# Repeated waits for a semaphore's value left out in an attention and FFN kernel

## The chip, the core and the metric

One NeuronCore of a Trainium2 chip runs the whole kernel. The metric is the device time of one execution in microseconds (us), lower is better. The engines are PE (TensorE), DVE (VectorE), ACT (ScalarE), POOL (GpSimd) and SP (SyncE, which here only issues DMAs). Each runs its own program, and they are ordered against each other by semaphores alone.

## What is computed

```python
# x: 2 x 1024 x 256, ctx: 2 x 77 x 256, all float32, 16 heads of 16
n   = layernorm(x)                                  # no scale, no shift
q   = n @ Wq + bq;  k = ctx @ Wk + bk;  v = ctx @ Wv + bv
att = 0.25 * q k^T per head
att = softmax(att * mask - 1e10 * (1 - mask))       # mask: 1 x 1 x 1024 x 77
x   = x + (att @ v) @ Wo + bo
n   = layernorm(x)
y   = n + relu(n @ w1[0] + b1[0]) @ w2[0] + b2[0]   # only expert 0 has weight
x   = x + layernorm(y) * gamma + beta
```

## The kernel before

The 2048 rows of x are worked off in four chunks of 512 rows (c = 0 to 3). A chunk goes through these kinds of steps: norm and scale (DVE, the first layernorm), turn (PE transposes, L557), qproj (the q projection, L573 and L574), smax (L643, 12 steps: scores with 128 rows of x as the stationary side, whose maximum over the 77 keys DVE takes at L978), mxt (the transposed maxima), st (L663, 16 steps, one a head: scores in the transposed layout, which ACT exponentiates at L824), pv (L675, four heads at a time), weigh, attn, proj (L702, L704, L707, the output projection), turn2 (L716), ffn1 (L725 to L727, 8 steps), ffn2 (L739, L740, L742, 8 steps), and result, root and finish (the last layernorm). A float32 operand that goes into a fast matmul is split into a high and a low part, so ffn1 and ffn2 use three matmuls for each product.

The order of the work is fixed. A table of planned times per engine (TIMES) lists every step, and walk(engine) returns that engine's steps sorted by it. So chunks overlap: while ffn1 and ffn2 of one chunk run, score steps of the next are put between them. Each engine's program loops over its walk and writes, in front of a step's instructions, a wait for each thing that the step needs: the semaphore and the value that it must have reached. The values come from the step's number (nth) and only grow. A step states all its needs, also those that an earlier step of the same engine has stated. A score step on PE reads:

```python
e.wait_ge(sq_ld[u % 2], 32 * (u // 2 + 1))
e.wait_ge(sq_static, 8 + 16 * (c // 2))
e.wait_ge(ks_made, 6)
e.wait_ge(ks_ident, 4)
if nth[step] > 2:
    e.wait_ge(exped, nth[step] - 2)
```

An engine instruction (a matmul, a copy, the issue of a DMA) can carry one wait itself. The others of the same step stand before it in separate semaphore instructions of the engine's sequencer, with up to two waits in each; the profile has them as EVENT_SEMAPHORE at the line of a wait (L660, L662 for the score step, L636, L637, L639 for smax, L671 and L673 for pv, L738 for ffn2, L540 for a PSUM bank that is taken).

SP's program issues the transfers: the first loads, and for each chunk quadq (L519: q of four heads, from the scratch tensor qD in DRAM, into four slots of the tile Sq), quadm (L528: the negated maxima, nmx, into one row of the same slots), qload (L510 and L512: q into the tile Mq), and qproj (L500, L502: the high and low part of q out to qD). masks (L493) loads the mask part of Sq once for the second half (1280 KB). Sq has two halves of four slots, and a half is loaded again once PE's scores have read it: this is the wait for st_made at L518 and L527. finish stores the result.

Of the kernel before, what the change touches and what calls it, by code (L numbers as in the profile page):

```python
# [211 lines left out]


# [6 lines left out]
def build(nc, x, ctx_in, mask, Wq, bq, Wk, bk, Wv, bv, Wo, bo, w1, b1, w2, b2, gamma, beta, const, out):  # L220
    stack = ExitStack()
    with stack:
# [236 lines left out]
        def sync_program(e):  # L459
            e.dma_start(xin[:, 0:4, :], x_v[:, 0:4, :]).then_inc(ld_x[0], 16)  # L460
# [9 lines left out]
            for step in walk("SP"):  # L470
# [11 lines left out]
                elif kind == "statics":  # L482
                    e.wait_ge(mT_made, 1)
                    e.dma_start(mD[:, :], mT[:, :].bitcast(F32)).then_inc(m_out, 16)
                elif kind == "maskm":
                    e.wait_ge(m_out, 16)
                    e.wait_ge(scored, 24)
                    e.dma_start(Mqf[0:QR, :, :], mD[:, 512:1024].unsqueeze(1).to_broadcast([QR, 6, 512])
                                ).then_inc(ms_static, 16)
                elif kind == "masks":  # L490
                    e.wait_ge(m_out, 16)
                    e.wait_ge(st_made, 32)
                    e.dma_start(Sqf[0:QR, :, :], mD[:, 512:1024].unsqueeze(1).to_broadcast([QR, 8, 512])  # L493
                                ).then_inc(sq_static, 16)
                elif kind == "qproj":
                    c, g = a
                    qd = qD[c][8 * g:8 * g + 8]
                    e.wait_ge(q_high, nth[step])
                    for r in (0, 2):
                        e.dma_start(qd[:, r, :, :], qh[:, g, :].bitcast(F32)).then_inc(q_out[g], 16)  # L500
                    e.wait_ge(q_split, nth[step])
                    e.dma_start(qd[:, 1, :, :], ql[:, g, :].bitcast(F32)).then_inc(q_out[g], 16)  # L502
                elif kind == "qload":
                    c, g = a
                    e.wait_ge(q_high, nth[step])
                    if c:

                        e.wait_ge(scored, 12 * (c - 1) + (12 if g else 8))
# [4 lines left out]
                elif kind == "quadq":  # L513
                    c, k = a
                    u, s = quad(c, k), 4 * (k % 2)
                    e.wait_ge(q_out[k // 2], 48 * (c + 1))
                    if u > 1:
                        e.wait_ge(st_made, 4 * (u - 1))  # L518
                    e.dma_start(Sqf[QR:P, s:s + 4, :],  # L519
                                qD[c][4 * k:4 * k + 4].rearrange("h r d n -> (r d) h n")).then_inc(sq_ld[u % 2], 16)  # L520
                elif kind == "quadm":
                    c, k = a
                    u, s = quad(c, k), 4 * (k % 2)
                    e.wait_ge(nmx_made, nth["mxt", c, k // 2])
                    if u > 1:
                        e.wait_ge(st_made, 4 * (u - 1))
                    e.wait_ge(sq_static, 8 + 16 * (c // 2))  # L527
                    e.dma_start(Sqf[MR:QR, s:s + 4, :], nmx[s:s + 4, k // 2, :].bitcast(F32)).then_inc(sq_ld[u % 2], 16)  # L528
                elif kind == "finish":
                    c, h, na, nb = a  # L530
                    n0 = row0(c) + 2 * h + na
                    e.wait_ge(y_done, nth[step])
                    e.dma_start(o_v[:, n0:n0 + nb - na, :], xn2[:, c % 2, 2 * h + na:2 * h + nb, :]).then_inc(stored[h], 16)
            for h in range(2):
                e.wait_ge(stored[h], 16 * (NC + 1))

        def tensor_program(e):
            def take(key):
                if free_when[key]:
                    e.wait_ge(*free_when[key])  # L540
                return bank[key]

            for step in walk("PE"):
                kind, a = step[0], step[1:]
                if kind == "rows":
                    e.wait_ge(ld_rows, 64)
                    e.wait_ge(ld_c, 16)
                    t = bank[step]
                    e.transpose(t[:, 0:14], rows[:, :], cst[0:14, 0:14]).then_inc(rows_turned, 1)
                elif kind == "turn":  # L550
                    c, = a
                    e.wait_ge(x_normed, nth["scale", c])
                    e.wait_ge(ld_c, 16)
# [5 lines left out]
                elif kind == "ctx":  # L559
                    e.wait_ge(ld_ctx, 16)  # L560
                    e.wait_ge(ld_c, 16)
# [6 lines left out]
                elif kind == "qproj":  # L568
                    c, g = a
                    e.wait_ge(xnT_made, 2 * nth["turn", c])  # L570
                    e.wait_ge(ld_wq, 16)
# [4 lines left out]
                elif kind == "kproj":  # L576
                    g, = a
                    e.wait_ge(ctx_made, 1)
                    e.wait_ge(ld_wk, 16)
# [5 lines left out]
                elif kind == "keys":  # L585
# [3 lines left out]
                    e.wait_ge(sel_made, 5)  # L589
                    e.wait_ge(low_ident, 1)  # L590
                    e.wait_ge(*((cols_made, 1), (ctx_made, 1), (v_copied, 1), (v_copied, 2), (mT_made, 1), (ks_made, 1),
                                (ks_made, 3), (ks_made, 4))[nth[step] - 1])
                    e.wait_ge(k_split, g + 1)
                    e.wait_ge(bqk_split, 1)
# [12 lines left out]
                elif kind == "bqk":  # L607
                    e.wait_ge(k_raw, 2)
                    e.wait_ge(bqh_made, 1)
# [5 lines left out]
                elif kind == "mask":  # L615
                    e.wait_ge(crow_made, 3)
                    e.wait_ge(identb_made, 1)
# [3 lines left out]
                elif kind == "values":  # L621
                    b, = a
                    e.wait_ge(ctx_made, 1)
                    e.wait_ge(ld_wv, 16)
# [3 lines left out]
                elif kind == "smax":  # L628
# [3 lines left out]
                    for g in (0, 1) if s == 2 else (s,):  # L632
                        e.wait_ge(ms_ld[g], 48 * (c + 1))
                    e.wait_ge(ms_static, 6 + 16 * (c // 2))
                    e.wait_ge(km_made, 6)
                    e.wait_ge(km_ident, 1)  # L636
                    e.wait_ge(ks_made, 2)  # L637
                    if nth[step] > 2:
                        e.wait_ge(maxed, nth[step] - 2)  # L639
# [6 lines left out]
                elif kind == "mxt":  # L646
                    c, g = a
                    e.wait_ge(maxed, 12 * c + (12 if g else 8))
# [4 lines left out]
                elif kind == "st":  # L653
# [3 lines left out]
                    e.wait_ge(sq_ld[u % 2], 32 * (u // 2 + 1))  # L657
                    e.wait_ge(sq_static, 8 + 16 * (c // 2))
                    e.wait_ge(ks_made, 6)
                    e.wait_ge(ks_ident, 4)  # L660
                    if nth[step] > 2:
                        e.wait_ge(exped, nth[step] - 2)  # L662
                    e.matmul(T[(nth[step] - 1) % 2][0:TK, :], KS[:, h, b, :], Sq[:, h % 8, :],  # L663
                             start=True, stop=True).then_inc(st_made, 1)
                elif kind == "pv":
# [3 lines left out]
                    e.wait_ge(exped, 4 * (u + 1))  # L669
                    e.wait_ge(v_copied, 2)  # L670
                    e.wait_ge(cleared, 3)  # L671
                    if u:
                        e.wait_ge(pv_copied, u)  # L673
# [4 lines left out]
                elif kind == "weigh":  # L678

                    c, k = a  # L680
                    e.wait_ge(pv_copied, nth[step])
# [4 lines left out]
                elif kind == "attn":  # L686
                    c, g = a
                    e.wait_ge(weighed, nth["weigh", c, 2 * g + 1])
# [4 lines left out]
                elif kind == "proj":  # L693
                    c, = a
                    e.wait_ge(wo_split, 1)
                    for h in range(2):
                        t = take(step + (h,))
                        for n in range(2):
                            q = (2 * h + n) * 128
                            for k in range(2):  # L700
                                e.wait_ge(a_high, nth["attn", c, k])
# [4 lines left out]
                                e.wait_ge(a_split, nth["attn", c, k])  # L706
# [3 lines left out]
                elif kind == "turn2":  # L710
                    c, = a
                    e.wait_ge(x2_normed, nth["scale2", c])
# [5 lines left out]
                elif kind == "ffn1":  # L718
                    c, f = a
                    e.wait_ge(x2_split, 2 * nth["turn2", c])  # L720
                    e.wait_ge(w1_split, 4)
# [7 lines left out]
                elif kind == "ffn2":  # L729
                    c, h, part = a  # L730
                    e.wait_ge(w2_split, 4)
# [5 lines left out]
                    for f in range(first, first + 4):  # L737
                        e.wait_ge(h_high, nth["ffn1", c, f])  # L738
                        e.matmul(y, hh[:, f, q:q + 128], w2h[:, f * E:(f + 1) * E], start=(f == 0), stop=False)  # L739
                        e.matmul(y, hh[:, f, q:q + 128], w2l[:, f * E:(f + 1) * E], start=False, stop=False)  # L740
                        e.wait_ge(*low_eng[c, f])
# [4 lines left out]
        def scalar_program(e):  # L746
            e.dma_start(ctx[:, :, :], ctx_in.rearrange("b t e -> t b e")).then_inc(ld_ctx, 16)
# [461 lines left out]
```

## Time and profile before

| | |
|---|---|
| median of 3 runs | 252.32 us |
| lowest and highest run | 250.85 and 252.41 us |
| profiled execution, first to last instruction (its span) | 250.3 us |
| the profiled execution's own time | only its span is given; the runs above are others |
| instructions in the span | 4118 |
| busy: PE, PE weight loads | 210.7 us (84%), 161.1 us (64%) |
| busy: DVE, ACT, POOL | 149.8 (60%), 121.3 (48%), 80.4 us (32%) |
| moved by DMA | 26.12 MB in 18101 packets |

The profile is of one execution. Busy time is that of the engine itself; time of its sequencer, on separate waits or on issuing a DMA, is not in it. Consecutive matmuls overlap in the records, so a matmul's duration is longer than the distance to the next; the chain of waits shows that distance. In the chain, "issue" is time for which the profile shows no wait, and a name with a q (SPq) is that engine's sequencer.

### The profile page before, as it was taken

To read this page: it belongs to the slowest core of one execution; us is meant where nothing else is said; L and a number is where in the kernel's file an instruction comes from. 1 tells how busy PE (TensorE), PEld (TensorE's weight loads), DVE (VectorE), ACT (ScalarE), POOL (GpSimd) and SP (SyncE) were. 2 spreads that over 40 slices of the span, in tenths; PEclk is the share of its full clock that TensorE was granted. 3 is DMA by queue.
4 is the path that set the end of the run, shared out by engine and by line. 5 is a ranking of instruction groups with operands and counts; after the bars stand their busy time and mean duration, and the time that the engine had idled before them with its cause. 6 is when DMAs were issued, how large, how long until landed. Compare 5 with 4: busy or idle time off the path is not lost.

```text
span 250.3 us, 4118 instructions
## 1 busy us (share of the span) xinstructions
PE 210.7 (84%) x1273; PEld 161.1 (64%) x1273; DVE 149.8 (60%) x354; ACT 121.3 (48%) x210; POOL 80.4 (32%) x88
## 2 busy tenths in 40 slices
PE   0378787687598687996999999999999999979990
PEld 0264765354434574474869776889677889968790
DVE  0988759764464477343136966745776426886464
ACT  2445921363376127768351547773646870149200
POOL 5629507310301031524121352241371341370010
PEclk9999955979799889999799999999999999999999
DMA  7962589347947636396044344000330100011011
GB/s 179 351 210 65 167 225 265 113 131 228 199 94 179 178 106 125 92 198 160 0 99 137 67 105 107 0 3 4 72 98 4 42 0 3 0 42 45 0 43 42
DMA packets 18101, 26.12 MB, mean 104 GB/s; under 512 B 2441, under 2 KB 9393, under 8 KB 18081
## 3 DMA queue, kind: packets, MB, share of 16 engines
q1 hardware_dynamic: 17200, 25.05, 38.8%
q10 hardware_dynamic: 881, 0.82, 1.3%
q8 instruction: 11, 0.18, 0.3%
q14 instruction: 9, 0.07, 0.1%
HBM read 14.92 MB, written 8.72 MB: 94 GB/s over the span
## 4 chain that ended last, share of the span: by engine, by line
PE 50%; DMA 18%; SPq 11%; DVE 11%; issue 7%; ACT 1%; POOL 1%; POOLq 0%; DVEq 0%
DMA Sq<-nmx 6%; PE W L725 5%; PE W L727 5%; PE W L726 5%; PE T L663 5%; DMA qD<-ql 4%; SPq L510 4%; PE W L742 4%; PE W L739 4%; PE W L740 4%; PE acc L675 4%; DMA Sq<-mD 3%; SPq L500 3%; PE W L557 2%; DMA Sq<-qD 2%
## 5 line engine op out<-in xcount | busy, mean ns | idle before, releaser
L824 ACT ACTIVATE PT<-T 77x512 f32<-77x512 f32 x64 | 35.2, 590 | 33.5 <-PE T L663 31.8
L739 PE MATMUL W<-w2h,hh 128*128 128x256 f32 x128 | 36.9, 288 | 0.4 <-ACT hh L868 0.4
L742 PE MATMUL W<-w2h,hl 128*128 128x256 f32 x128 | 36.4, 285 | 0.2 <-DVE hl L1041 0.2
L740 PE MATMUL W<-w2l,hh 128*128 128x256 f32 x128 | 36.3, 283 | 0.0
L978 DVE TENSOR_REDUCE mx<-M 128x6 f32<-128x462 f32 (+1 forms) x48 | 26.3, 581 | 15.4 <-PE M L643 14.6
L663 PE MATMUL T<-Sq,KS 128*77 128x512 f32 x64 | 25.4, 456 | 5.3 <-DMA Sq<-nmx 3.0
L864 ACT ACTIVATE hr<-W,cols 128x512 f32<-128x512 f32 x32 | 22.0, 688 | 14.3 <-PE W L727 13.1
L725 PE MATMUL W<-x2h,w1h 128*128 128x512 f32 x64 | 26.5, 414 | 1.5 <-DVE x2l L1035 1.5
L1159 POOL TENSOR_TENSOR hl<-hr,hh 128x512 fp32r<-128x512 f32 x12 | 15.5, 1288 | 34.7 <-ACT hh L868 34.7
L1041 DVE TENSOR_TENSOR hl<-hr,hh 128x512 fp32r<-128x512 f32 x20 | 14.5, 727 | 20.1 <-ACT hh L868 20.0
L643 PE MATMUL M<-KM,Mq 128*128 128x234 f32 (+1 forms) x96 | 21.0, 337 | 6.4 <-issue 2.3
L739 PEld LDWEIGHTS W<-w2h,hh 128*128 128x128 f32 x128 | 24.5, 192 | 2.1 <-issue 0.8
L727 PE MATMUL W<-x2h,w1l 128*128 128x512 f32 x64 | 25.7, 402 | 0.0
L726 PE MATMUL W<-x2l,w1h 128*128 128x512 f32 x64 | 25.6, 400 | 0.0
L643 PEld LDWEIGHTS M<-KM,Mq 128*128 128x128 f32 (+1 forms) x96 | 17.2, 229 | 12.7 <-issue 8.4
L740 PEld LDWEIGHTS W<-w2l,hh 128*128 128x128 f32 x128 | 24.5, 191 | 0.6
L742 PEld LDWEIGHTS W<-w2h,hl 128*128 128x128 f32 x128 | 24.4, 191 | 0.4 <-DVE hl L1041 0.4
L1129 POOL TENSOR_TENSOR xin<-xin,bo_r 128x512 f32<-128x512 f32 x8 | 10.6, 1342 | 37.4 <-DVE xn L916 37.4
L868 ACT CAST hh<-hr 128x512 fp32r<-128x512 f32 x32 | 19.8, 620 | 1.0
L1165 POOL TENSOR_TENSOR rs<-ve,mh 128x2 f32<-128x2 f32 (+1 forms) x10 | 6.4, 641 | 42.3 <-DVE ve L1062 42.1
L663 PEld LDWEIGHTS T<-Sq,KS 128*77 128x77 f32 x64 | 9.2, 155 | 14.9 <-issue 8.4
L675 PE MATMUL acc<-PT,Vb 77*32 77x512 f32 x128 | 17.2, 610 | 0.0
(138 smaller groups left out, 413.5 us busy)
## 6 DMA issues: line engine op xcount, KB each, us to landing
Sq<-qD SPq DMA_DIRECT2D x16, 384.0 KB
qD<-qh SPq DMA_DIRECT2D x16, 256.0 KB
xin<-in_x_dram SPq DMA_DIRECT2D x4, 512.0 KB, 9.4
qD<-ql SPq DMA_DIRECT2D x8, 256.0 KB
Mq<-qh SPq DMA_DIRECT2D x16, 96.0 KB, 3.8
out_dram<-xn SPq DMA_DIRECT2D x6, 256.0 KB, 2.4
Sq<-mD SPq DMA_DIRECT2D x1, 1280.0 KB, 8.2
w1raw<-in_L_ffn_w_dram SPq DMA_DIRECT2D x2, 512.0 KB, 8.8
```

What stands on the lines that cost most here:

```text
L643: i = e.matmul(m[:, j * w * KP:(j + 1) * w * KP], Mq[0:r, 2 * s + j, n * 128:(n + 1) * 128], KM[0:r, h0:h0 + w, b, :], start=True, stop=True)
L663: e.matmul(T[(nth[step] - 1) % 2][0:TK, :], KS[:, h, b, :], Sq[:, h % 8, :], start=True, stop=True).then_inc(st_made, 1)
L675: i = e.matmul(acc[32 * j:32 * j + 32, :], Vb[:, b, 4 * k + j, :], PT[:, (4 * u + j) % 6, :], start=True, stop=True, tile_position=(0, 32 ...
L725: e.matmul(t[:, :], w1h[:, o:o + 128], x2h[:, k, :], start=(k == 0), stop=False)
L726: e.matmul(t[:, :], w1h[:, o:o + 128], x2l[:, k, :], start=False, stop=False)
L727: i = e.matmul(t[:, :], w1l[:, o:o + 128], x2h[:, k, :], start=False, stop=(k == 1))
L739: e.matmul(y, hh[:, f, q:q + 128], w2h[:, f * E:(f + 1) * E], start=(f == 0), stop=False)
L740: e.matmul(y, hh[:, f, q:q + 128], w2l[:, f * E:(f + 1) * E], start=False, stop=False)
L742: i = e.matmul(y, hl[:, f, q:q + 128], w2h[:, f * E:(f + 1) * E], start=False, stop=(f == 7))
L824: e.activation(PT[:, m % 6, :], T[m % 2][0:TK, :], ACT.Exp).then_inc(exped, 1)
L864: e.activation(hr[:, r, :], bank[step][:, :], ACT.Relu, bias=cols[:, 6 + f:7 + f]).then_inc(relu_made, 1)
L978: e.tensor_reduce(heads, M[(nth[step] - 1) % 2][:, 0:w * KP].rearrange("p (g h t) -> p g h t", g=1 if s < 2 else 2, t=KP)[:, :, :, 0:TK], ...
```

## The change

Each of the five programs makes one object of a new class, and all its waits go through it. It keeps, per semaphore, the highest value that this engine has waited for, and emits a wait only for a higher one.

```diff
+class Fresh:
+    def __init__(self, engine):
+        self.engine, self.settled = engine, {}
+
+    def wait_ge(self, signal, value):
+        if self.settled.get(signal.name, 0) < value:
+            self.settled[signal.name] = value
+            self.engine.wait_ge(signal, value)
...
         def tensor_program(e):
+            fresh = Fresh(e)
             def take(key):
                 if free_when[key]:
-                    e.wait_ge(*free_when[key])
+                    fresh.wait_ge(*free_when[key])
                 return bank[key]
...
                 elif kind == "st":
                     c, h = a
                     b, u = CHUNKS[c][0], quad(c, h // 4)
-                    e.wait_ge(sq_ld[u % 2], 32 * (u // 2 + 1))
-                    e.wait_ge(sq_static, 8 + 16 * (c // 2))
-                    e.wait_ge(ks_made, 6)
-                    e.wait_ge(ks_ident, 4)
+                    fresh.wait_ge(sq_ld[u % 2], 32 * (u // 2 + 1))
+                    fresh.wait_ge(sq_static, 8 + 16 * (c // 2))
+                    fresh.wait_ge(ks_made, 6)
+                    fresh.wait_ge(ks_ident, 4)
                     if nth[step] > 2:
-                        e.wait_ge(exped, nth[step] - 2)
+                        fresh.wait_ge(exped, nth[step] - 2)
```

The same replacement is made at every other wait of the five programs (184 lines in all). The steps, their order, the instructions that compute and the DMAs are the same.

## Rows read from the trace of the kernel before

**Rows 1.** The page: busy tenths of PE in 40 slices, and ACT's exponentials.
```profile
PE   0378787687598687996999999999999999979990
...
L824 ACT ACTIVATE PT<-T 77x512 f32<-77x512 f32 x64 | 35.2, 590 | 33.5 <-PE T L663 31.8
```
**Rows 2.** Windows: start:end, length, busy us of each engine, clock, DMA share, GB/s.
```profile
24.00:64.00 40.00, 30.01 (x164) 20.68 (x164) 25.35 (x52) 17.29 (x32) 12.95 (x13) 0.79 0.68 186
119.20:123.20 4.00, 3.98 (x14) 3.42 (x15) 0.00 (x0) 1.73 (x3) 0.42 (x1) 0.58 0.00 0
123.20:204.00 80.80, 80.80 (x536) 64.27 (x535) 49.77 (x116) 47.69 (x84) 26.07 (x22) 1.00 0.24 57
```
**Rows 3.** The chain of waits over the whole span, longest pieces: start, us, what.
```profile
29.85 7.61 DMA qD<-ql
39.08 1.97 PE W L557 x8
...
84.55 7.02 DMA Sq<-nmx
```
**Rows 4.** The chain of waits from 71 to 85 us.
```profile
72.62 0.05 issue
72.67 0.02 SPq L508
72.68 0.03 issue
...
73.28 0.05 issue
...
78.04 2.18 SPq L510
```
**Rows 5.** The chain of waits from 123 to 204 us: shares by line.
```profile
by line: PE W L725 10.1%; PE acc L675 9.8%; PE W L727 9.8%; PE W L726 9.7%; PE W L739 9.6%; PE W L742 9.5%; PE W L740 9.5%; PE T L663 9.4%; PE W L684 4.6%; PE M L643 3.4%; PE W L702 2.6%; PE W L704 2.4%; PE W L707 2.4%; PE W L716 2.2%; PE W
```
**Rows 6.** Instructions at PE's wait lines: duration min/median/max, first and last start.
```profile
L636 PEldq EVENT_SEMAPHORE  x48: 51/51/51, 29.1 to 163.6; - x48
L637 PEldq EVENT_SEMAPHORE  x48: 51/51/51, 29.2 to 163.7; - x48
L660 PEldq EVENT_SEMAPHORE  x64: 51/51/51, 49.7 to 186.5; - x64
```
**Rows 7.** Timeline of PE from 145.2 to 146.7 us: start, duration, instruction.
```profile
145.62 0.28 PE L739 MATMUL W<-w2h,hh 128*128 128x256 f32 x1
145.74 0.28 PE L740 MATMUL W<-w2l,hh 128*128 128x256 f32 x1
145.86 0.29 PE L742 MATMUL W<-w2h,hl 128*128 128x256 f32 x1
```
**Rows 8.** PE's groups from 123 to 204 us: busy, mean ns, idle before.
```profile
L740 PE MATMUL W<-w2l,hh 128*128 128x256 f32 x64 | 18.1, 283 | 0.0
L727 PE MATMUL W<-x2h,w1l 128*128 128x512 f32 x34 | 13.4, 395 | 0.0
```
**Rows 9.** The chain of waits from 119 to 125 us.
```profile
120.71 0.43 PE W L725
...
122.20 0.21 PE W L740
...
123.43 0.12 PE W L740
...
124.71 0.23 PE W L727
```
**Rows 10.** SP's waits from 24 to 119 us: total, times, longest.
```profile
SPq L527 <- PE T L663: 20.0, 2, 13.2
SPq L518 <- PE T L663: 11.8, 2, 9.9
```
**Rows 11.** Timeline of PE around 119 us, with the idle time before.
```profile
119.22 0.45 PE L663 MATMUL T<-Sq,KS 128*77 128x512 f32 x1 [2.33 <-DMA Sq<-nmx]
```
**Rows 12.** The chain of waits from 96 to 104 us.
```profile
101.87 0.87 PE W L716 x8
```

More of the change, by code:

```diff
@@ L504, in sync_program @@
                     c, g = a
-                    e.wait_ge(q_high, nth[step])
+                    fresh.wait_ge(q_high, nth[step])
                     if c:
-                        e.wait_ge(scored, 12 * (c - 1) + (12 if g else 8))
+                        fresh.wait_ge(scored, 12 * (c - 1) + (12 if g else 8))
                     for j in range(2):
@@ L632, in tensor_program @@
                     for g in (0, 1) if s == 2 else (s,):
[L633 to L637, printed above, removed]
+                        fresh.wait_ge(ms_ld[g], 48 * (c + 1))
+                    fresh.wait_ge(ms_static, 6 + 16 * (c // 2))
+                    fresh.wait_ge(km_made, 6)
+                    fresh.wait_ge(km_ident, 1)
+                    fresh.wait_ge(ks_made, 2)
                     if nth[step] > 2:
-                        e.wait_ge(maxed, nth[step] - 2)
+                        fresh.wait_ge(maxed, nth[step] - 2)
                     w, r = (3, 128) if s < 2 else (2, 112)
@@ L680, in tensor_program @@
                     c, k = a
-                    e.wait_ge(pv_copied, nth[step])
+                    fresh.wait_ge(pv_copied, nth[step])
                     t = take(step)
@@ L765, in scalar_program @@
                     n = len(range(r, 8, 3))
-                    e.wait_ge(keys_made, nth[step])
+                    fresh.wait_ge(keys_made, nth[step])
                     e.activation(KM[64:P, 8 * g + r:8 * g + 8:3, :, 0:TK],
@@ L786, in scalar_program @@
                     c, g = a
-                    e.wait_ge(q_made, nth[step])
+                    fresh.wait_ge(q_made, nth[step])
                     if c:
-                        e.wait_ge(q_out[g], 48 * c)
-                    e.wait_ge(x_turned, 2 * nth["turn", c])
+                        fresh.wait_ge(q_out[g], 48 * c)
+                    fresh.wait_ge(x_turned, 2 * nth["turn", c])
                     e.copy(qh[:, g, :], bank[step][:, :]).then_inc(q_high, 1)
@@ L899, in vector_program @@
                     i.then_inc(x_stat, 1)
-                    e.wait_ge(x_stat, nth[step])
+                    fresh.wait_ge(x_stat, nth[step])
                     for n in range(4):
@@ L903, in vector_program @@
                     i.then_inc(x_aggr, 1)
-                    e.wait_ge(x_aggr, nth[step])
+                    fresh.wait_ge(x_aggr, nth[step])
                     e.tensor_scalar(ve[:, :], mv[:, :, 1], EPS, None, ALU.add).then_inc(x_var, 1)
@@ L927, in vector_program @@
                 elif kind == "qproj":
-                    e.wait_ge(q_high, nth[step])
+                    fresh.wait_ge(q_high, nth[step])
                     c, g = a
                     if c:
-                        e.wait_ge(q_out[g], 48 * c)
+                        fresh.wait_ge(q_out[g], 48 * c)
                     e.tensor_tensor(ql[:, g, :], bank[step][:, :], qh[:, g, :].bitcast(F32),
@@ L943, in vector_program @@
                     n = len(range(r, 8, 3))
-                    e.wait_ge(keys_made, nth[step])
+                    fresh.wait_ge(keys_made, nth[step])
                     if to == "both":
-                        e.wait_ge(km_made, nth[step])
+                        fresh.wait_ge(km_made, nth[step])
                     e.tensor_scalar(KS[64:P, 8 * g + r:8 * g + 8:3, :, :],
@@ L966, in vector_program @@
                     if w == 2:
-                        e.wait_ge(w_high, nth[step])
+                        fresh.wait_ge(w_high, nth[step])
                         e.tensor_tensor(w2l[:, 512 * k:512 * k + 512], w2raw[:, 512 * k:512 * k + 512],
@@ L972, in vector_program @@
                     w = 6 if s < 2 else 4
-                    e.wait_ge(scored, nth[step])
+                    fresh.wait_ge(scored, nth[step])
                     if c:
-                        e.wait_ge(mx_turned, 2 * (c - 1) + (2 if s else 1))
+                        fresh.wait_ge(mx_turned, 2 * (c - 1) + (2 if s else 1))
                     heads = mx[:, n, :].rearrange("p (g h) -> p g h", g=2)
@@ L994, in vector_program @@
                     c, g = a
-                    e.wait_ge(a_high, nth[step])
+                    fresh.wait_ge(a_high, nth[step])
                     e.scalar_tensor_tensor(aTl[:, g, :], bank[step][:, :], cols[:, 4 + g:5 + g], aT[:, g, :].bitcast(F32),
@@ L1009, in vector_program @@
                     i.then_inc(x1_stat, 1)
-                    e.wait_ge(x1_stat, nth[step])
+                    fresh.wait_ge(x1_stat, nth[step])
                     for n in range(4):
@@ L1013, in vector_program @@
                     i.then_inc(x1_aggr, 1)
-                    e.wait_ge(x1_aggr, nth[step])
+                    fresh.wait_ge(x1_aggr, nth[step])
                     e.tensor_scalar(ve[:, :], mv[:, :, 1], EPS, None, ALU.add).then_inc(x1_var, 1)
@@ L1033, in vector_program @@
                     for k in range(2):
-                        e.wait_ge(x2_high, 2 * (nth[step] - 1) + k + 1)
+                        fresh.wait_ge(x2_high, 2 * (nth[step] - 1) + k + 1)
                         e.tensor_tensor(x2l[:, k, :], bank[step + (k,)][:, :], x2h[:, k, :].bitcast(F32),
@@ L1060, in vector_program @@
                     i.then_inc(y_aggr, 1)
-                    e.wait_ge(y_aggr, nth[step])
+                    fresh.wait_ge(y_aggr, nth[step])
                     e.tensor_scalar(ve[:, na:nb], mv[:, na:nb, 1], EPS, None, ALU.add).then_inc(y_var, 1)
@@ L1072, in vector_program @@
                     i.then_inc(y_centred, 1)
-                    e.wait_ge(y_centred, nth[step])
+                    fresh.wait_ge(y_centred, nth[step])
                     for n in range(na, nb):
@@ L1136, in gpsimd_program @@
                     if w == 1:
-                        e.wait_ge(w_high, nth[step])
+                        fresh.wait_ge(w_high, nth[step])
                         e.tensor_tensor(w1l[:, 512 * k:512 * k + 512], w1raw[:, 512 * k:512 * k + 512],
@@ L1163, in gpsimd_program @@
                     st, mv, ve, rs = stats[1 + h]
-                    e.wait_ge(y_var, nth[step])
+                    fresh.wait_ge(y_var, nth[step])
                     e.tensor_tensor(rs[:, na:nb], ve[:, na:nb], mh[:, na:nb], ALU.pow).then_inc(y_rstd, 1)
```

300 lines of the change are left out of this document (152 added, 148 removed).

## The prediction

> **What bounds the kernel now.** The page first. PE is busy for 84% of the span, but its slices say that the kernel has two halves [rows 1]: up to about 119 us PE is broken, from there to about 218 us PE stands at 9 tenths in every slice. The windows make that sharp [rows 2]: of the 80.8 us from 123.2 to 204 PE is busy for all of them at the full clock, with a DMA share of 0.24; of the 40 us from 24 to 64 it is busy for 30.0 at a mean clock of 0.79, with a DMA share of 0.68.
>
> Next, what the time of the first half hangs on. The longest pieces of the chain that ended last [rows 3] are transfers: a store of q of 7.61 us and, of four loads that follow each other between 84.5 and 119.2 us, the first with 7.02. What lies between them is mostly SP's queue: from 71.6 to 84.5 the chain runs through one DMA issue after the other, up to 2.18 us each [rows 4]. PE is on the chain before 119 us only for some 18 us (about 39 to 45, 65 to 72, 92 to 94, 99.6 to 103.2).
>
> In the second half the chain is PE alone: from 123 to 204 us it names only lines of PE, without an "issue" piece and without another engine among its large shares, and its longest pieces are rows of matmuls merged at their regular pace [rows 5].
>
> **What the change removes.** An instruction carries one wait. Further waits in front of it ride in separate semaphore instructions, up to two in each, that the engine's sequencer runs one by one. A score step (L663) has five waits and thus two separate ones. The trace has them, one of the two at L660 (64 of them), and for the max scores those at L636 and L637 (48 each) [rows 6]. I went through each engine's waits in program order with the rule of the diff, "skip when this engine has waited for that value or a higher one", and packed what is left in the same way. PE keeps 68 of 446 separate waits, so 378 go (7 before 24 us, 201 from there to 119, 156 to 218, 14 behind). ACT loses 96 of 165, DVE 64 of 111, POOL 14 of 22, SP 25 of 40. Waits that ride in an instruction go too (on PE 267 of 553). No compute instruction or DMA is added, removed or moved, and no new wait is made.
>
> **What each is worth.** *PE, time of the sequencer.* A separate wait whose value has been reached lasts 51 ns, and the next follows about 0.1 us after it started (L636 first at 29.1 and L637 at 29.2, last at 163.6 and 163.7) [rows 6]. So 378 of them are about 38 us of PE's sequencer, and that is the upper bound; the lower is 0, if it always runs ahead. From 123.2 us on, the rows say that it does. There the ffn2 matmuls of L739 and L742, which carry a wait, and of L740, which never does, follow each other at the same 0.12 us [rows 7], and PE has no idle time before any line [rows 8].
>
> How much can be hidden in that pace? In the 81 us of [rows 5] the shares of L725, L726 and L727 are 10.1, 9.8 and 9.7%, 24.0 us; 34 of each [rows 8] at 0.23 us, the pace of [rows 9] once the clock is full, make 23.5. For L739, L740 and L742 they are 28.6%, 23.2 us, against 192 at 0.12 = 23.0. So some 0.7 us of irregular spacing lies in these two groups, less than half of it next to a separate wait. I take 0.4 us for this stretch and 0.1 for the end, with 0 and 1.5 as the bounds.
>
> *PE, where it resumes after a wait.* After the loads of the first half, L663 already waits in the instruction itself for the transfer, so nothing is gained there. Where the wait for DVE's max stands in a separate one (L639), PE comes back a little later, but PE idles for that only before 55 us, beside the DMA queue and off the chain: 0, and at most one separate wait's 0.1 us for each of a few such stops.
>
> *SP.* Here the chain itself shows the price. Between two DMA issues stand 0.05 us (at 73.28); with a separate wait between them 0.05 + 0.02 + 0.03 = 0.10 [rows 4]. A removed one gives 0.05 us. Nine of the 25 stand on the chain (48.5, 72.0, 72.7, 76.7, 83.2, 84.5, 94.4, 103.2 and 112.3 us): 0.4 us. Bounds: 0, if the DMA rings set the pace and an earlier issue only takes longer, and 0.45. What covers them otherwise is SP's wait for PE or for a transfer.
>
> *ACT, DVE, POOL.* ACT's stand between exponentials of 590 ns, which wait for PE for 31.8 us in all [rows 1]. DVE's and POOL's stand likewise in front of a wait for another engine. I take 0, bounds 0 and 0.2; the cover is PE's stream in the second half and the transfers in the first.
>
> Here a rule speaks against the change. The Trainium skill, VectorE: DVE Perf Modes, section The DRAIN you can't avoid, has eight copies with a semaphore after each take as long as with one after the last: a semaphore costs nothing extra. Carried to all queues, it would make the sum 0 and the time 252.3; SP's rows above speak of 0.05 us each, so I don't carry it to SP.
>
> **The sum.** 0.5 + 0.4 = 0.9 us off a span of 250.3, giving 249.4. The runs were 250.85 to 252.41 with a median of 252.32, some 2.0 us over the profiled span. I keep those 2.0: 252.3 - 0.9 = **251.4 us**. A difference under 1% (2.5 us) counts as none for a measurement of this kernel, whose own three runs lie 0.6% apart.
>
> **Rivals.**
> *A, SP waits less for PE (faster).* SP waits for PE's scores before it may load: 20.0 and 11.8 us before 119 us [rows 10], four waits. 201 of PE's separate waits go there. If the scores that end these waits come 0.7 us earlier each, seven separate waits' time, the loads start earlier: 3 us more, 248.4 us. Against it: what stands in front of these scores on the chain is a transfer, not PE.
> *B, a low clock goes away (faster).* From 119.2 to 123.2 us PE's mean granted clock is 0.58, so mostly the 1.2 GHz level, after PE had stood idle for 2.33 us [rows 2, 11]. The matmuls there take 0.21 and 0.43 instead of 0.12 and 0.23 us [rows 9]: 1.5 us. At 39 to 45 us the same eight transposes take 1.97 us against 0.87 at 101.9 [rows 3, 12]. If one such stretch on the chain goes, 1.5 to 3 us: 249.2 us. Against it: the idle time before them is a wait for DMA, which stays. The Trainium skill, TensorE: Matmul & The Clock Gate, section on psum-queue depth-cycling, has short idles between groups of matmuls bring the low clock back. By that rule fewer sequencer gaps would help; the rows show no idle time in the second half for it to remove.
> *C, one more low clock (slower).* The sequencer gets through its work sooner and PE stands idle longer before the loads of 84 to 119 us, so that the clock falls, or comes back later, at another moment: just where the stream starts. Price by the same rows 1.5 us for a stretch like 119.2 to 123.2, on top of which the gain of 0.9 is lost where the loads only shift. One gives 252.3 + 1.5 - 0.4 = 253.4 us, two 254.9. It decides as soon as the added low clock on the chain costs more than 0.9 us. For it: where the clock falls is sensitive to small shifts, and the runs of before spread by 1.56 us. Against it: no idle time is added in the stream itself.
> *D, nothing is taken out.* If the same instructions were left (waits packed otherwise), 252.3 us. The trace has 64 at L660 alone, after whose first all are repeats, so this is unlikely.
>
> **How the numbers follow.** Forecast 0.55, A 0.15, B 0.10, C 0.17, D 0.03. Faster by over 1% (under 249.8): nearly all of A, half or more of B and 0.02 of the forecast, 0.22. Slower by over 1% (over 254.8): half of C, 0.08. Within 1%: 0.70. The forecast's own range is 250.2 (all upper bounds of the costs but the 38 us, which the pace excludes) to 252.6 (no gain, spread of the runs). The range for 8 in 10 reaches to half of A and to C with one stretch: 248.0 to 253.8.
>
> **What would show it.** Right: PE's semaphore instructions fall from 447 to about 69, L636 and L637 vanish and L660, L662 nearly; the ffn2 matmuls still come every 0.12 us; the stream from 119 to 218 us is at most 1 us shorter; SP's issues follow at 0.05 us; the transfers of 7 to 8 us stand where they were. Wrong: if L663 and L643 come faster in the first half and loads start over 1 us earlier (A), if the low-clock slices are others (B, C), or if the ffn2 matmuls come closer than 0.12 us, which would mean that a carried wait costs PE time after all.

## The result, and the profile of the changed kernel

Over 20 runs of each kernel the changed one takes 253.61 us (median; 249.94 to 256.87), the one before 251.80 (248.02 to 255.04). The ratio is 1.0077 [1.0039, 1.0115]: slower, by some 0.8%, where 251.4 us and a small gain were forecast. The ratio leaves out of each kernel the runs far above that kernel's own fastest one, and because both kernels spread by 7 us this cuts each differently; so medians, and below the means of all runs, stand beside it. Here the means lie 1.97 us apart, with a standard error of 0.5; every error below is such a standard error. The profiled execution of the changed kernel took 249.94 us with a span of 248.1, the fastest of its 20. Its end is no picture of the median; a second profiled execution of the same instructions (span 253.1 us) is shown for that.

The page of the changed kernel, first of that fast execution: PE's busy tenths, its granted clock, and ACT's exponentials.

```profile
PE   0289886699688958995999999999999999989990
...
PEclk9999965956997999999799999999999999999996
...
L839 ACT ACTIVATE PT<-T 77x512 f32<-77x512 f32 x64 | 35.2, 590 | 34.5 <-PE T L677 32.9
```

Against [rows 1] the picture is the same: a broken first half, a full second one, and the same exponentials. The clock row of the kernel before, which [rows 1] leaves out, is

```profile
PEclk9999955979799889999799999999999999999999
```

Its last slice, where PE has next to nothing left to do, stands at 9 tenths and here at 6. A mean clock over the whole span counts such a slice too. The count of instructions falls from 4118 to 3545, so by 573. What is left of separate waits stands at one line, that of the new class (L224); here it is by engine, with durations (min/median/max) and first and last start.

```profile
L224 ACTq EVENT_SEMAPHORE  x69: 17/17/38, 15.5 to 229.0; - x69
L224 PEldq EVENT_SEMAPHORE  x66: 51/51/51, 5.7 to 225.1; - x66
L224 DVEq EVENT_SEMAPHORE  x47: 21/21/3194, 26.1 to 232.5; - x47
L224 SPq EVENT_SEMAPHORE  x15: 17/17/17, 39.4 to 247.7; - x15
L224 POOLq EVENT_SEMAPHORE  x8: 17/17/43, 4.2 to 203.0; - x8
```

So the change does what it says; the repeats of [rows 6] are gone. Windows of the same execution (start:end, length, busy us of PE, its weight loads, DVE, ACT, POOL, then clock, DMA share, GB/s):

```profile
24.00:64.00 40.00, 31.51 (x166) 21.31 (x164) 26.61 (x55) 18.01 (x33) 13.13 (x13) 0.74 0.70 189
...
117.10:121.30 4.20, 4.20 (x17) 3.74 (x18) 0.41 (x1) 1.90 (x3) 0.14 (x1) 0.62 0.02 4
...
124.00:204.00 80.00, 80.00 (x538) 63.88 (x537) 49.45 (x115) 47.51 (x83) 27.05 (x23) 1.00 0.23 57
```

These answer [rows 2]: the low clock at the start of the stream is still there, and a little lower in the mean from 24 to 64 us. PE's timeline in three places: the first matmul of the stream, the ffn2 matmuls inside it, the last one.

```profile
117.06 0.46 PE L677 MATMUL T<-Sq,KS 128*77 128x512 f32 x1 [2.54 <-DMA Sq<-nmx]
...
143.45 0.28 PE L753 MATMUL W<-w2h,hh 128*128 128x256 f32 x1
143.57 0.28 PE L754 MATMUL W<-w2l,hh 128*128 128x256 f32 x1
143.69 0.28 PE L756 MATMUL W<-w2h,hl 128*128 128x256 f32 x1
...
241.88 0.28 PE L756 MATMUL W<-w2h,hl 128*128 128x256 f32 x1
```

And the last one of the kernel before:

```profile
244.04 0.28 PE L742 MATMUL W<-w2h,hl 128*128 128x256 f32 x1
```

The reader is to see two things. The ffn2 matmuls keep their 0.12 us, as in [rows 7]. And the stream as a whole, 117.06 to 241.88, is 124.82 us; before it was 119.22 [rows 11] to 244.04, also 124.82. The waits removed from PE inside it were worth nothing, and what follows its last matmul is as long as before, 6.2 us. The whole 2.2 us by which this span is shorter lies ahead of the stream.

There the chain of waits of the changed kernel reads (start, us, what):

```profile
30.98 6.56 DMA qD<-ql
...
39.16 1.97 PE W L571 x8
...
73.56 0.04 issue
73.60 0.71 SPq L515
74.31 0.04 issue
74.36 1.34 SPq L523
75.70 0.04 issue
75.74 2.20 SPq L523
...
81.97 7.19 DMA Sq<-nmx
...
99.54 0.87 PE W L730 x8
...
109.12 7.89 DMA Sq<-nmx
...
119.48 0.21 PE W L753
...
121.75 0.12 PE W L756
```

It answers [rows 3, 4, 9, 12]: SP's issues now follow each other at 0.04 us; the eight transposes still take 1.97 and 0.87 us; the ffn2 matmuls still come at 0.21 us and then at 0.12. The store of q is 6.56 us here. Now the chain of the second execution of the same instructions, with a span of 253.1:

```profile
31.07 9.00 DMA qD<-ql
...
41.69 1.97 PE W L571 x8
...
114.28 7.80 DMA Sq<-nmx
...
122.13 0.71 PE T L677
```

Its last matmul, from the timeline:

```profile
246.87 0.28 PE L756 MATMUL W<-w2h,hl 128*128 128x256 f32 x1
```

From 122.13 to 246.87 are 124.74 us again. So between two executions of one kernel the stream starts 5.07 us apart and lasts the same; 2.4 us of the 5.07 are one store that lands later. In these two executions the whole difference is made ahead of the stream.

### The profile page after: what moved, and what is told of

It is laid out like the page before. It is cut to its first block, busy times and chain, and to the rows that moved or that the text cites. A ratio compares the mean times of both kernels' runs of the same rounds, so it can differ in the third digit from the quotient of the medians.

```text
span 248.1 us, 3545 instructions
## 1 busy us (share of the span) xinstructions
PE 211.0 (85%) x1273; PEld 160.6 (65%) x1273; DVE 150.3 (61%) x354; ACT 121.3 (49%) x210; POOL 80.3 (32%) x88
## 4 chain that ended last, share of the span: by engine, by line
PE 51%; DMA 20%; SPq 13%; DVE 9%; issue 3%; ACT 1%; POOL 1%; POOLq 0%; DVEq 0%
DMA Sq<-nmx 9%; PE W L739 5%; PE W L741 5%; PE W L740 5%; SPq L523 5%; PE T L677 5%; PE W L756 4%; PE W L753 4%; PE W L754 4%; SPq L513 4%; DMA qD<-ql 4%; PE acc L689 4%; DMA Sq<-mD 3%; DMA Sq<-qD 2%; PE W L587 2%
## 5 line engine op out<-in xcount | busy, mean ns | idle before, releaser
L657 PE MATMUL M<-KM,Mq 128*128 128x234 f32 (+1 forms) x96 | 21.6, 346 | 3.9 <-DMA Mq<-qh 2.6
L657 PEld LDWEIGHTS M<-KM,Mq 128*128 128x128 f32 (+1 forms) x96 | 18.2, 241 | 10.0 <-DMA Mq<-qh 3.6
L689 PE MATMUL acc<-PT,Vb 77*32 77x512 f32 x128 | 18.0, 634 | 0.0
```

The lines of the kernel that those rows point to most:

```text
L657: i = e.matmul(m[:, j * w * KP:(j + 1) * w * KP], Mq[0:r, 2 * s + j, n * 128:(n + 1) * 128], KM[0:r, h0:h0 + w, b, :], start=True, stop=True)
L689: i = e.matmul(acc[32 * j:32 * j + 32, :], Vb[:, b, 4 * k + j, :], PT[:, (4 * u + j) % 6, :], start=True, stop=True, tile_position=(0, 32 ...
```

## The experiments

Medians, means and granted clocks are those of all timed runs (12 of a kernel if nothing else is said). Kernels that ran on one chip share the runs of the kernel before: e1 to e4 had before at 251.70 (mean 251.59, 35 runs), e5 to e8 at 252.01 (252.11, 29 runs), e9 to e12 at 251.96 (251.53, 17), e13 to e16 at 252.41 (252.62, 23), e17 and e18 at 251.90 (252.22, 23).

### Which engine's waits

**e1_all**: the changed kernel again. No edit.

> The changed kernel again, all five programs skip repeated waits. The measured pair was 1.0077 of before. If that holds it comes out 1 to 3 us slower than before here too; if the pair was drift between executions it comes out within 0.5 us.

Measured: 253.75 us, mean 253.34, ratio 1.0055 [0.9988, 1.0123]. By the means the slowdown is there in a second set of runs too, 1.75 us (error 0.6); the interval of the ratio just takes in 1.

**e2_pe_only**: the other four programs wait as before.

```diff
 def sync_program(e):      # the same in scalar_, vector_ and gpsimd_program
-    fresh = Fresh(e)
+    fresh = e
```

> Only PE's program skips repeated waits (378 separate waits fewer), the other four wait as before. Clock theory: PE gets through its work sooner, stands idle longer before loads and works more of the path at the low clock, so this alone brings the 2 us, and the mean granted clock is lower than before's. SP theory: within 0.5 us of before.

Measured: 252.83 us, mean 252.48, ratio 0.9963 [0.9914, 1.0013]. Median and mean are about 1 us above before (means 0.9, error 0.7), the ratio is below 1; alone it decides nothing.

**e3_sp_only**: only SP leaves repeats out.

```diff
 def tensor_program(e):    # the same in scalar_, vector_ and gpsimd_program
-    fresh = Fresh(e)
+    fresh = e
```

> Only SP's program skips repeated waits (25 fewer). SP theory: transfers are issued closer together or at other moments and one on the path lands later, so this alone brings about 2 us. Clock theory: 0.4 us faster than before, the 0.05 us of nine removed waits on the path.

Measured: 249.28 us, mean 250.26, ratio 0.9930 [0.9891, 0.9970]: faster, by 1.3 us between the means (error 0.6), and by the ratio by more than the 0.4 us of my sum.

**e4_act_dve_pool**: SP and PE wait as before.

```diff
 def sync_program(e):      # the same in tensor_program
-    fresh = Fresh(e)
+    fresh = e
```

> Only ACT, DVE and POOL skip repeated waits. Both theories: within 0.5 us of before. If it is 2 us slower, both are wrong and the cause lies in an engine that I had put at nothing.

Measured: 253.17 us, mean 253.11, ratio 1.0076 [1.0033, 1.0118]: slower by 1.5 us between the means (error 0.5), where I had costed nothing.

**e5_act_only, e6_dve_only, e7_pool_only**: one of these three each.

```diff
 # e5: in all programs but scalar_program, e6: but vector_program, e7: but gpsimd_program
-    fresh = Fresh(e)
+    fresh = e
```

> Only ACT skips repeated waits (96 separate waits fewer, 58 of them between exponentials). The three of ACT, DVE and POOL together were 1.0076 of before. Theory ACT: the exponentials and copies come at other moments, and this alone is 1 to 2 us slower. Theory DVE or POOL: within 0.5 us of before. Theory chance: all three single ones within 0.5 us.

> Only DVE skips repeated waits (64 fewer, 30 of them before the maxima). Theory DVE: DVE starts its maxima and low parts sooner and this alone is 1 to 2 us slower; otherwise within 0.5 us of before.

> Only POOL skips repeated waits (12 to 14 fewer). No theory gives it more than 0.3 us either way; a difference here would say that the spread of the runs makes up the others too.

Measured: ACT 251.97 (mean 252.01 without one run of 1078.84), ratio 1.0009 [0.9962, 1.0057]; DVE 252.98 (mean 252.12, 6 runs), ratio 0.9893 [0.9811, 0.9976]; POOL 252.05 (mean 252.28), ratio 1.0020 [0.9979, 1.0060]. By the means none of the three moves the time by over 0.2 us, with errors of 0.7, 1.0 and 0.5. Their sum is 0.1 us with an error of 1.5, too wide to say whether the 1.5 us of e4 (error 0.5) are the sum of these parts or something that only the three together bring.

**e8_pe_sp**: PE and SP leave repeats out.

```diff
 def scalar_program(e):    # the same in vector_ and gpsimd_program
-    fresh = Fresh(e)
+    fresh = e
```

> PE and SP skip repeated waits, the others wait as before. Adding up the single ones in their means (SP -1.3, PE +0.9 us): 251.2, 0.4 us faster than before. If ACT, DVE and POOL are the cause of the slowdown, it is faster than the changed kernel by 1.5 to 2 us. Clock theory: its mean granted clock is as low as the changed kernel's (0.938), because PE's part is in.

Measured: 252.26 us, mean 251.98, ratio 0.9957 [0.9904, 1.0010]. With PE's part beside it, SP's gain is no longer to be seen (0.1 us under before by the means, error 0.5).

A least-squares fit to the 124 timed runs of before, e1 to e4 and e8 on their two chips, with one term each for PE, SP and the other three and one common level for both chips, gives PE +1.1 us, SP -1.1, the other three +1.5, each with an error of 0.4; with a level of its own for each chip the last is +1.7. The sum, +1.5, is close to the 1.8 between the medians of the result. The fit takes the parts to add up, which no run shows, and PE's part alone (e2) is not clear of noise: the term of PE rests on all five kernels together.

**What the profiles of these show.** Windows of the first 4.2 us of the stream, e3_sp_only:

```profile
117.90:122.10 4.20, 4.15 (x24) 3.67 (x25) 0.69 (x1) 2.50 (x4) 0.85 (x1) 1.00 0.00 0
```

e4_act_dve_pool:

```profile
121.70:125.90 4.20, 4.16 (x24) 3.68 (x25) 0.69 (x1) 2.50 (x4) 0.45 (x1) 1.00 0.00 0
```

e2_pe_only:

```profile
119.80:124.00 4.20, 4.20 (x16) 3.55 (x17) 0.00 (x0) 1.49 (x3) 0.45 (x1) 0.60 0.01 4
```

The third number from the end is the clock. It is 1.00 in e3 and e4, the 2.4 GHz level throughout, and 0.60 in e2, mostly the 1.2 GHz level: in the same time 16 matmuls start, not 24. The timelines give the length of the stream, here e3 and then e2:

```profile
117.95 0.45 PE L677 MATMUL T<-Sq,KS 128*77 128x512 f32 x1 [1.94 <-DMA Sq<-nmx]
...
241.24 0.28 PE L756 MATMUL W<-w2h,hl 128*128 128x256 f32 x1
```

```profile
119.76 0.71 PE L677 MATMUL T<-Sq,KS 128*77 128x512 f32 x1 [2.24 <-DMA Sq<-nmx]
...
244.62 0.28 PE L756 MATMUL W<-w2h,hl 128*128 128x256 f32 x1
```

123.3 us without a low clock at its start, 124.9 with one: 1.5 to 1.6 us, the price that [rows 9] gave. All five profiles of kernels with PE's part (the changed kernel twice as result and e1, once as e12, then e2 and e8) have it, at 0.59 to 0.66. Of those with PE's waits kept, only that of before has it (0.59 from 119.2 to 123.4 us), and e3, e4, e5, e6 and e7 do not. Five of five against one of six, each a single execution.

The timed runs carry a mean granted clock each. Kernels with PE's part have 0.938, 0.941 and 0.941 (e1, e2, e8), those without 0.943 to 0.947, before 0.946 to 0.947. The same fit for the clock gives PE -0.006 with an error of 0.002. One low start costs 0.40 of 4.2 us, or 1.7 us of full clock; over 250 us that is 0.0067. So the clock that PE's part loses is what one such stretch more in nearly every execution would take. It need not be at this place, though: the mean also counts low time elsewhere, and that at the end of the span, where it costs nothing. In the windows from 24 us to the start of the stream the clock is 0.86 to 0.87 in the five profiles with PE's part and 0.86 to 0.89 in the six without.

### Is it the clock

If the clock is the cost, keeping PE busy before those waits should take it away. I put transposes of the identity, written to a PSUM bank that is free then, ahead of the wait in five places. They only add work and, ahead of it, the wait that makes the bank free. For turn the wait for the constants moves ahead of the transposes.

**e9_before_busy**: the kernel before, with these.

```diff
+fill = {("turn", 1): 10, ("turn", 2): 14, ("smax", 1, 0, 0): 10, ("st", 1, 4): 12, ("st", 2, 0): 14}
+def keep_busy(step, t):
+    for _ in range(fill.get(step, 0)):
+        e.transpose(t[:, 0:128], ident, ident)
...
+                    if step in fill:        # st; turn and smax likewise
+                        e.wait_ge(exped, nth[step] - 2)
+                        keep_busy(step, T[(nth[step] - 1) % 2])
                     e.wait_ge(sq_ld[u % 2], 32 * (u // 2 + 1))
```

> The kernel before, with dummy transposes of 128 columns (their result is overwritten) on PE just before five of its waits: 10 and 14 before the transposes of chunks 1 and 2, 10 before the max scores of chunk 1, 12 and 14 before the score steps (1, 4) and (2, 0). They fill part of PE's idle time. Clock theory: fewer low-clock stretches on the path, mean clock up by 0.01, time 1 to 3 us under before. SP theory: no change, or up to 1 us slower from the dummies.

Measured: 248.75 us, mean 248.79, ratio 0.9931 [0.9872, 0.9990], mean clock 0.966. Faster than before by 2.7 us between the means (error 0.7), with 60 more transposes on PE. Its clock row and its windows:

```profile
PEclk9999997979999999999999999999999999999996
```

```profile
24.00:64.00 40.00, 31.70 (x205) 22.75 (x204) 28.07 (x59) 17.90 (x33) 14.11 (x14) 0.91 0.75 194
64.00:119.00 55.00, 49.69 (x291) 32.94 (x290) 27.85 (x68) 34.71 (x62) 15.68 (x14) 1.00 0.61 141
```

From 24 to 64 us the clock is 0.91 in place of 0.79 [rows 2], behind that it is full, and the ffn1 matmuls at the stream's start (114.76 us) come at 0.23 us from the first on.

**e10_all_busy**: the changed kernel with the same five places (6 runs), and **e16_all_busy_again**: the same on another chip (6 runs).

```diff
 class Fresh:              # kept, in all five programs
...
+fill = {("turn", 1): 10, ("turn", 2): 14, ("smax", 1, 0, 0): 10, ("st", 1, 4): 12, ("st", 2, 0): 14}
```

> The changed kernel with the same dummy transposes. Clock theory: PE's part of the slowdown (about 1 us) came from its longer idle time before the waits, so that this kernel is at most 0.5 us over the kernel before with dummies, and 2 to 4 us under the changed one; the low clock at the start of the stream is gone. Rival: still 1.5 to 2 us over the kernel before with dummies.

> The changed kernel with dummies at five places, again, for more runs (it had six: 250.3 and a mean of 249.3 us). Clock theory: at most 0.5 us over the kernel before with dummies, so 248.0 to 249.3. Rival: 250.3 or more, which is the whole 1.5 to 2 us over it.

Measured: e10 250.30 us, mean 249.28, ratio 0.9853 [0.9763, 0.9943], clock 0.967; e16 249.63, mean 249.68, ratio 0.9856 [0.9794, 0.9917], clock 0.964. Against the changed kernel's 253.4, on other chips, this is a gain of 4 us. e10 lies 0.5 us over e9 by the means of one chip, where the kernels without the transposes lie 1.75 us apart; with six runs of e10 the error of the 0.5 is 1.2, so this pair does not tell the two apart. Its median of 250.30 lies 1.55 over that of e9.

**e11_sp_busy**: SP's part alone, with the five places (6 runs).

```diff
 def tensor_program(e):    # the same in scalar_, vector_ and gpsimd_program
-    fresh = Fresh(e)
+    fresh = e
+    fill = {("turn", 1): 10, ("turn", 2): 14, ("smax", 1, 0, 0): 10, ("st", 1, 4): 12, ("st", 2, 0): 14}
```

> Only SP skips repeated waits, with the dummy transposes: the best of both if SP's gain of 1.3 us and the clock's add up. Expected 247.5 to 249.5 us, under the kernel before and the changed one.

Measured: 247.37 us, mean 248.26, ratio 0.9897 [0.9838, 0.9956]. By the means it lies 0.5 us under e9 (error 0.9): in the direction of e3, but no gain is shown.

**e12_all_look**: the changed kernel once more, for a profile that is not of its fastest run. No edit.

> The changed kernel once more, one profile of an ordinary execution, since both profiles so far are of its fastest executions. Clock theory: a low-clock stretch at the start of the stream (about 1.5 us), and others where PE resumes after a load. SP theory: a transfer between 60 and 117 us that lands 2 to 4 us later than in the two profiles so far.

Measured: 254.95 us, span 253.1. This is the second execution read above, on another chip than e1.

**e13_all_busy_st** and **e14_before_busy_st**: only the 14 transposes ahead of the stream, in the changed kernel and in the one before.

```diff
-fill = {("turn", 1): 10, ("turn", 2): 14, ("smax", 1, 0, 0): 10, ("st", 1, 4): 12, ("st", 2, 0): 14}
+fill = {("st", 2, 0): 14}
```

> The changed kernel with 14 dummy transposes at one place only, ahead of the score step (2, 0), where the stream of the second half starts. In all five profiles with PE's part of the change a low-clock stretch lies there, in the six without it only in one. Clock theory: 1 to 1.5 us under the changed kernel, about 252. If the five are chance of alignment: 0.3 to 0.7 us under it.

> The kernel before with the same 14 dummies at that one place. If the low clock falls there seldom in it: within 0.5 us of before. If as often as in the changed kernel: 1 to 1.5 us under before.

Measured: e13 252.06 us, mean 252.07, ratio 0.9999 [0.9962, 1.0037]; e14 252.03, mean 252.05, ratio 0.9969 [0.9924, 1.0014]. With PE kept busy at this one place the whole change costs 0.0 us between the means of one chip (error 0.5), where it cost 1.97 and 1.75 (errors 0.5 and 0.6) without; between the two ratios some 0.3% are left of 0.8 and 0.6%. PE's timeline in e13:

```profile
119.22 1.69 PE L561 MATMUL T<-cst 128*128 128x128 f32 x14
121.97 0.45 PE L691 MATMUL T<-Sq,KS 128*77 128x512 f32 x1 [1.07 <-DMA Sq<-nmx]
...
245.22 0.28 PE L770 MATMUL W<-w2h,hl 128*128 128x256 f32 x1
```

The transposes fill 1.69 us of the wait, and the stream is 123.25 us long, with PE's repeats left out. e3, which keeps them, has 123.29. That is the measure of what they were worth there: under 0.1 us.

Two figures speak against laying PE's whole part to this one place. e14, which keeps PE's waits, is 0.6 us under before too (error 0.5), near the first case of its expectation, that of a low clock that falls there seldom, but not clear of the second. And the mean clock of e13's runs is 0.940 where those of e14 and of before on this chip have 0.945, with no low clock at the start of the stream in either profile: a deficit of 0.005 (error 0.003), about that of e2 and e8. The low time then lies elsewhere, and in single executions it moves about a good deal. From 24 us to the start of the stream, e13 and then e14:

```profile
24.00:121.90 97.90, 75.66 (x424) 49.23 (x422) 54.82 (x124) 50.54 (x91) 29.03 (x27) 0.90 0.65 158
```

```profile
24.00:122.80 98.80, 79.77 (x424) 51.89 (x422) 54.80 (x124) 50.70 (x91) 28.43 (x27) 0.84 0.64 157
```

Here the kernel with PE's waits kept has the lower clock, 0.84.

**e15_rest_busy** (ACT, DVE and POOL leave out, five places, 6 runs), **e17_rest_busy_st** (the same with the one place), **e18_sp_rest_busy** (SP too, five places): is the cost of e4 one of the clock too?

```diff
 def tensor_program(e):    # e15 and e17: the same in sync_program
-    fresh = Fresh(e)
+    fresh = e
...
+    fill = {("turn", 1): 10, ("turn", 2): 14, ("smax", 1, 0, 0): 10, ("st", 1, 4): 12, ("st", 2, 0): 14}   # e17: {("st", 2, 0): 14}
```

> ACT, DVE and POOL skip repeated waits, with the dummies at all five places. These three together were 1.5 us over before (n of 12) and their mean clock was not lower. If their slowdown comes by the clock all the same, 248.5 to 249.5 us like the kernel before with dummies (248.75); if it is a transfer's or an engine's own, 250 us or more.

> ACT, DVE and POOL skip repeated waits, with 14 dummies only ahead of the score step (2, 0). If the 1.5 us of these three come from the low clock at the start of the stream too, it comes to the level of the kernel before with these dummies, 0 to 0.5 us under before. If they come from elsewhere in the first half, it stays 1 to 1.5 us over before.

> All but PE skip repeated waits, with the dummies at all five places: the parts that cost no clock, and the clock held up. Expected the lowest of all, 246 to 248.5 us, 1.5% or more under before. If it is over 249, the low time of the three with dummies (246.95 from six runs) was chance.

Measured: e15 246.95 us, mean 247.63, ratio 0.9780 [0.9713, 0.9847], clock 0.970; e17 252.55, mean 252.38, ratio 1.0094 [1.0044, 1.0143], clock 0.951; e18 248.28, mean 248.25, ratio 0.9842 [0.9790, 0.9893], clock 0.971. With the five places nothing is seen of a cost of the three engines' part (e15 lies 1.2 us under e9 by the means, on another chip and from six runs). With the one place the ratio still shows it and the mean (0.2 us over before) hardly does, so e17 doesn't settle where it lies. e15 and e18 are the versions furthest below before in all runs, and faster than the changed kernel as well. e18 keeps PE's waits and is 1.2 us below e10 and e16 (means 248.25 and some 249.5, on different chips; error 0.8): a loss by PE's part with PE kept busy is possible, but not clear of noise.

## Why the prediction was wrong

**What was removed: right.** 577 instructions were expected to go and 573 went; 66, 69, 47, 15 and 8 separate waits are left, against 68, 69, 47, 15 and 8. Rival D falls.

**The steps that failed: two terms of the sum.** They are PE's, "I take 0.4 us for this stretch and 0.1 for the end", which leaves out any loss by the clock, and that of ACT, DVE and POOL, put at 0 (further below). For PE's the bounds were 0 and 1.5, and in the stream it is the lower bound: 124.82 us before and after, 123.29 and 123.25 in the pair without the low clock. The sequencer's waits are hidden behind PE all the way. The 0.7 us of irregular spacing that I read out of [rows 5, 8] is not of the waits, as the stream is as long without them. Measured over whole executions PE's part has the other sign, +1.1 us (error 0.4) in place of -0.5, and goes with a lower mean clock, by 0.006 (error 0.002). With the clock held fixed in the fit +0.3 us (error 0.3) are left of it.

**Rival C: right in kind for PE's part, too low in chance.** Its price of 1.5 us for a low stretch at the stream's start is what the timelines give. That its 253.4 us lies by the 253.61 measured is in part luck: it started from 252.3, the median of three runs of before, where twenty have 251.80, and the rise measured holds 1.5 us of ACT, DVE and POOL that C knows nothing of. I gave it 0.17 because "no idle time is added in the stream itself". That was the wrong place to look: the low stretch stands behind the idle time ahead of it, 1.9 to 2.5 us in the rows above, which is there with and without the repeats. Shown are a lower mean clock with PE's part, the price of one low stretch, and, by 0.0 us (error 0.5) against 1.97 and 1.75, that the loss of the whole change shrinks or goes when PE is kept busy ahead of the stream. Not shown is by what link fewer waits on the sequencer bring a low clock. In e2's profile the idle time before the stream is 2.24 us, in e3's 1.94, in e4's 2.32 (a full clock there), so its length alone doesn't sort them. And with five profiles against six, of which the profile of before is an exception, and with e13's mean clock still at 0.940, the place is less certain than the mean clock. Nor was it tried to put other instructions in the place of the waits: leaving them out also makes the programs shorter (20 packets of instruction loads on q8 and q14 before, 17 after), and no run tells that from the sequencer's time.

The Trainium skill, TensorE: Matmul & The Clock Gate, section on psum-queue depth-cycling, blames short idles between groups of matmuls for a clock that comes and goes. Taken as a rule for this edit, fewer gaps of the sequencer should have raised the clock. The runs have it 0.006 lower, so the rule does not carry over to waits that leave no gap on PE. The section HAM oscillation of the same page blames waits for DMA between short pieces of work. The trace agrees in part: in before the low stretch stands behind such a wait of 2.33 us, and the transposes put into five waits raised the mean clock from 0.948 to 0.966. But in e4 a wait of 2.32 us is followed by the full clock, and the work behind it is no short piece.

**SP: right in mechanism, too small.** The issues follow at 0.04 us where 0.10 stood with a separate wait. The chain gives 0.4 us. The fit gives 1.1 (error 0.4), e3 a ratio of 0.9930 [0.9891, 0.9970], and e11 against e9 0.5 (error 0.9). If more comes of it than the chain holds, that would fit loads that start earlier at a better moment, but this was not separated.

**Rival A falls.** The run with PE's part alone tests it, by one profile. Here are SP's waits in e2 up to the stream (total, times, longest), the same ones as in [rows 10]:

```profile
SPq L540 <- PE T L677: 20.1, 2, 13.0
SPq L531 <- PE T L677: 12.7, 2, 9.4
```

They were 20.0 and 11.8. SP did not wait less for PE's scores; in this execution it waited 1 us more.

**ACT, DVE, POOL: wrong.** I took 0 and bounded a gain by 0.2 us, and did not bound a loss at all. It was +1.5 us (error 0.4) together on one chip, and 0.2 or less singly on another (errors 0.5 to 1.0). With PE's part it makes up the miss, in about equal shares. Holding the clock fixed in the fit leaves +1.2 of it, so it is mostly not the clock of PE. With the five places it isn't seen. The cause stays open. Its place would be ahead of the stream, as the stream of e4 is 123.32 us long (121.74 to 245.06), as short as e3's, and starts 3.8 us later. But the starts of single executions say little here: those of e6 and e7 are at 121.74 and 121.35, with no cost in the means.

**Sum.** Forecast and result lie 2.7 us apart against before (-0.9 and +1.8). PE's part makes 1.6 of it, the three engines 1.5, SP -0.7: 2.4. Rival B's stretch did not go away by the change, only by the transposes; e9 shows that it was worth having.

**The range** and the 0.70 for within 1% hold the result; the side was wrong, and 253.61 lies close to the upper end of 253.8.

## What to carry to other kernels

Here a wait for a value already reached cost nothing in front of an engine that is never idle, so look for its price first on the queue that stands on the chain, here SP's. Ahead of a long stretch of matmuls ask what the clock is when it starts: an edit that saves sequencer time on PE can lose more by a low clock than it saves, and idle time spent on throwaway transposes gained more (e9, 248.75 us; e18, 248.28) than the edit under study could. If executions of one kernel spread by 7 us, compare many runs of both on one chip, and in the traces the length of a fixed stretch, not spans: the spans of one kernel lay at 248.1 and 253.1 us around the same 124.8. A mean clock helps, but it also counts low time that costs nothing. And take an engine's part at nothing only with a bound on both sides: the term that was given no possible loss made half of the miss.

## What was not expected of the hardware

Between two executions of the same instructions the same store of q landed after 6.56 and after 9.00 us. Work added to an engine made the kernel faster: 60 transposes took 2.7 us off (error 0.7). And leaving out waits that the trace shows to be hidden in full in the stream went with a mean granted clock lower by 0.006 (error 0.002).
